# Performer layer: the half squares of the queries issued in two parts, the first ahead of the last query projection, the second behind the first tile's features

## What is computed

```python
def softmax_kernel(x, proj, is_query):
    norm = x.shape[-1] ** (-0.25)
    ratio = proj.shape[0] ** (-0.5)
    xp = jnp.einsum('bhnd,md->bhnm', x * norm, proj)
    diag = jnp.sum(jnp.square(x), axis=-1, keepdims=True) * 0.5 * (norm * norm)
    if is_query:
        stab = jnp.max(xp, axis=-1, keepdims=True)
    else:
        stab = jnp.max(xp, axis=(-1, -2), keepdims=True)
    return ratio * (jnp.exp(xp - diag - stab) + EPS_K)
...
qp = softmax_kernel(q, proj, is_query=True)
kp = softmax_kernel(k, proj, is_query=False)
k_sum = jnp.sum(kp, axis=2)
denom = jnp.einsum('bhnm,bhm->bhn', qp, k_sum)
ctx = jnp.einsum('bhnm,bhnd->bhmd', kp, v)
out = jnp.einsum('bhnm,bhmd->bhnd', qp, ctx) / denom[..., None]
```

## Time and profile before

| what | value |
|---|---|
| median of 3 runs | 2508.66 us |
| lowest and highest run | 2501.77 and 2509.47 us |
| the profiled execution's own time | 2511.11 us |
| its span | 2509.4 us |
| PE busy | 2360.6 us, 94% of the span |
| DVE, ACT, POOL busy | 1791.1, 1291.6, 701.0 us (71, 51, 28%) |
| mean granted clock of PE over the span | 0.97 of full speed |

### The profile page before, as it was taken

The page is one execution under the profiler, slowest core; times in us unless marked ns, Lnnn a source line. Parts: engine busy times, 40 slices in busy tenths (PEclk is TensorE's granted clock), DMA queues, the critical chain, the costliest instruction groups (busy, mean ns, idle before and its releaser), DMA issues.

```text
span 2509.4 us, 43786 instructions
## 1 busy us (share of the span) xinstructions
PE 2360.6 (94%) x16024; PEld 2182.2 (87%) x16024; DVE 1791.1 (71%) x3323; ACT 1291.6 (51%) x2027; POOL 701.0 (28%) x468
## 2 busy tenths in 40 slices
PE   7999995899999969999999999998999999999999
PEld 6888885899999968988988988987988998899998
DVE  5776775899999866565575574665788787877774
ACT  4445443344444325464464554564666665655554
POOL 1111111444454423023123122122344442321110
PEclk9999997999999989999999999996999999999999
DMA  5000000000000000000000000002000010000001
GB/s 182 0 0 0 0 0 20 1 0 0 0 0 0 1 17 1 13 8 13 13 4 17 13 4 17 8 13 81 26 18 22 20 50 28 1 26 26 25 25 34
DMA packets 43259, 45.69 MB, mean 18 GB/s; under 512 B 3120, under 2 KB 41904, under 8 KB 43184
## 3 DMA queue, kind: packets, MB, share of 16 engines
q1 hardware_dynamic: 43184, 44.69, 5.5%
HBM read 27.90 MB, written 16.78 MB: 18 GB/s over the span
## 4 chain that ended last, share of the span: by engine, by line
PE 51%; DVE 5%; issue 3%; ACT 2%; POOL 1%; DVEq 0%; ACTq 0%; POOLq 0%
PE m_ps_z L1859 12%; PE p_ps_a L1641 4%; PE p_ps_feat L279 4%; PE p_ps_a L1698 4%; PE p_ps_feat L281 3%; PE p_ps_feat L280 3%; PE m_ps_wide L279 3%; PE m_ps_wide L281 3%; PE m_ps_wide L280 3%; PE p_ps_a L1579 2%; PE p_ps_turn L1685 2%; PE m_ps_wide L1837 1%; PE m_ps_wide L1838 1%; PE m_ps_n L1820 1%; PE p_ps_b L279 1%
## 5 line engine op out<-in xcount | busy, mean ns | idle before, releaser
L1951 DVE TENSOR_TENSOR m_a_lo<-m_a,m_a_hi 128x512 fp32r<-128x512 f32 x256 | 201.2, 803 | 144.0 <-ACT m_a_hi L1911 140.1
L1859 PE MATMUL m_ps_z<-m_w_hi,m_a_hi 128*128 128x256 f32 x1024 | 290.7, 284 | 1.5 <-DVE m_a_lo L1951 0.9
L1859 PE MATMUL m_ps_z<-m_w_hi,m_a_lo 128*128 128x256 f32 x1024 | 288.0, 281 | 0.0
L1859 PEld LDWEIGHTS m_ps_z<-m_w_hi,m_a_hi 128*128 128x128 f32 x1024 | 192.3, 188 | 13.5 <-DVE d_w_lo L2468 1.9
L1859 PEld LDWEIGHTS m_ps_z<-m_w_hi,m_a_lo 128*128 128x128 f32 x1024 | 192.7, 188 | 0.0
L1907 ACT ACTIVATE m_a<-m_ps_wide,d_b,d_w_gain 128x512 f32<-128x512 f32 x128 | 99.8, 780 | 135.8 <-PE m_ps_wide L281 131.7
L1324 POOL TENSOR_TENSOR p_kf<-p_kf,p_k_shift 128x1024 f32<-128x1024 f32 x64 | 119.4, 1903 | 155.5 <-DVE p_k_shift L1459 155.5
L1859 PE MATMUL m_ps_z<-d_w_lo,m_a_hi 128*128 128x256 f32 x512 | 144.7, 283 | 0.0
L1859 PE MATMUL m_ps_z<-m_w_lo,m_a_hi 128*128 128x256 f32 x512 | 143.6, 280 | 0.0
L1641 PE MATMUL p_ps_a<-p_ctx_pair,p_kf 128*128 128x34 f32 x1024 | 128.4, 283 | 0.0
L1641 PEld LDWEIGHTS p_ps_a<-p_ctx_pair,p_kf 128*128 128x128 f32 x1024 | 127.7, 203 | 0.4
(11 more groups left out here) (350 smaller groups left out, 8027.4 us busy)
## 6 DMA issues: line engine op xcount, KB each, us to landing
residual<-in_x SPq DMA_DIRECT2D x8, 1024.0 KB, 11.8
attn<-p_attn SPq DMA_DIRECT2D x32, 256.0 KB, 2.2
m_attn<-attn SPq DMA_DIRECT2D x16, 512.0 KB, 3.8
out<-residual SPq DMA_DIRECT2D x16, 512.0 KB, 2.9
raw_weights<-in_d_q SPq DMA_DIRECT2D x2, 1024.0 KB, 7.2
m_attn<-in_d_scale SPq DMA_DIRECT2D x3, 512.0 KB, 4.0
raw_weights<-in_m_w1T SPq DMA_DIRECT2D x1, 1024.0 KB, 5.0
raw_weights<-in_m_w2T SPq DMA_DIRECT2D x1, 1024.0 KB, 7.9
```

The costliest lines, as they stand in the source:

```text
L1859: mm = pe.matmul(z, a, w[:, f, :], start=(f == 0 and k == 0 and j % 2 == 0), stop=(f == FC - 1 and k == 2), skip_group_check=True)
L1951: dve.tensor_tensor(self.a2[1][:, f, :], self.a[f % RING][:, :], self.a2[0][:, f, :].bitcast(F32), ALU.subtract).then_inc(self.a_lo, 1)
```

## The change

In the tail of the Performer layer PE's program is reordered. The first half of the queries' half squares (rows of fills 0 and 1) is issued before the last query projection, the second half (fills 2 and 3) behind the features of tile 0. The wait for the keys' half squares to have been copied moves with the first half. Tile 0's features now wait for the low parts of fills 0 and 1 alone (`kq_lo` at b * 8 + 6) and tile 1's for all four, where both waited for all four. DVE's, ACT's, POOL's and SP's programs are the same.

```diff
@@ -1666,17 +1666,18 @@
                 project("q", 2)
                 pe.wait_ge(stab_ready, b + 1)
                 pe.matmul(ps_b[:, 0:HEADS], ones[:, :], stab_diag[:, :], start=True, stop=True).then_inc(stab_spread, 1)
+                pe.wait_ge(halfsq_copied, 2 * b + 1)
+                half_squares(b, ps_a, 1, 0)
                 project("q", 3)
-                pe.wait_ge(halfsq_copied, 2 * b + 1)
-                for half in range(2):
-                    half_squares(b, ps_a, 1, half)
                 for i in range(TB + 2):
                     if i < TB:
                         if i < 2:
-                            pe.wait_ge(kq_lo, b * 8 + 8)
+                            pe.wait_ge(kq_lo, b * 8 + 6 + 2 * i)
                         else:
                             pe.wait_ge(q_shifted, b * TB + i - 1)
                         features(i).then_inc(qf_done, 1)
+                    if i == 0:
+                        half_squares(b, ps_a, 1, 1)
                     if i >= 2:
                         pe.wait_ge(q_exp, b * TB + i - 1)
                         if i >= 3:
```

## The result

| | before | after |
|---|---|---|
| median of 12 runs | 2508.22 us | 2513.53 us |
| lowest and highest | 2501.77, 2509.99 | 2511.99, 2514.82 |
| profiled execution, its span | 2511.11, 2509.4 | 2513.51, 2511.8 |

The account below looks back on a forecast made before the run. PE, busy 94% of the span, was read as the bound, with tile 0's add held to POOL's boundaries; +1.86 + 1.86 - 1.87 - 0.53 = +1.3 us on 2508.66 gave 2510.0 us, "same"; range 2503 to 2517.

Parts of the forecast that it names:

- Nothing to take away on PE: PE through one tail: no wait there for the reorder to remove; same matmuls, same 6.5 us sum.
- PE waits 0.1 us: Tile 0's features just cover ACT's square of fill 3; if short, PE waits 0.1 us.
- DVE 0.33 us later: Tile 0's maximum on DVE starts at 1080.47 instead of 1080.14 us, held by the copy of both halves.
- First boundary missed, second reached: Tile 0's add ends at POOL subtraction boundaries (7.9, 9.8, 11.6 us after `k_shift`); ready at 8.00, it ends at 9.8.
- The rival in which the second is missed: Low-clock tails: tile 0's add goes to the third boundary, +1.86 us each; 2517.4 with four, 2521.2 with six; chance 0.12.
- that in which the first is caught: Tile 0's add starts at or before 7.87 us: 2495.1 in all eight tails, 2502.6 in four; chance 0.07.
- Clock: PE's clock behind the half squares falls less often than in six of eight tails; bounds none and six, four taken.
- new idle time: Rival: PE waits for tile 0's subtraction, clock falls, 0.53 us per batch, 2512.1; chance 0.2 together with no boundary matters.
- The sum: All eight tails at the second boundary against the profiled execution: +1.86 + 1.86 - 1.87 - 0.53 = +1.3 us.
- the median: Last step: profiled execution 2.45 us above the median of three runs, so median put at 2508.66 + 1.3 = 2510.0 us.
- such an execution: An execution like the profiled one before the change: 2511.11 + 1.3 = 2512.4 us forecast.

Follow-up runs that it names:

- the pair of doses: Three PSUM copies delaying DVE, added to the kernel with first half squares behind projection 3: 2515.24 to 2513.16 us (half squares in SBUF), 2493.65 to 2502.50 (in PSUM).

## Why the prediction was right, and where it was off

*Nothing to take away on PE.* Right: no wait went, one of 0.13 us came, as the "PE waits 0.1 us" had it.

*DVE 0.33 us later.* Right in sign and cause (the copy in one piece behind both halves; shown by the run with the copy in two), short in size: 8.21 against 7.67 in b = 1 is 0.54. The wait of 0.13 is a part of it, and from the copy's start to the maximum's it is 0.42 us, not 0.29 + 0.04.

*First boundary missed, second reached.* Right in all eight tails; with the low clock the add was ready at 9.54, where 9.59 was forecast. That agreement is luck: 9.59 was for a clock that falls behind all the half squares, and the 9.54 came of one that fell during projection 3. The rival in which the second is missed did not come about, nor that in which the first is caught: the order with the first half squares behind projection 3, ready at 7.98, shows how near that was. The mechanism, that the add is held by POOL and the hold is all of a step, is shown by the runs with one SBUF input and by the pair of doses.

*Clock.* A fall early in the tail came in two tails, not the four that I took, within the bounds of none and six, and behind the first half squares, not behind the second; and the "new idle time" rival was real as well: in b = 0, 3 and 6 the clock fell as PE waited for tile 0's subtraction, which cost 0.3 us in each distance (96.9 against 96.6 for b = 0 and 3, 96.2 against 95.9 for b = 6), where I had 0.53.

*The sum.* +1.3 us between profiled executions; measured 2513.51 - 2511.11 = +2.4. The first mark came 0.4 us earlier. From the first mark to the last it is 0.3 us less (676.79 to 676.51), where 1.86 - 1.87 - 0.53 = -0.5 was forecast. Two things are missing in that sum: the 0.3 us of b = 0 and 3, and b = 6, which I had as unchanged. It had the same extra 0.53 before as b = 2 (96.48 against 95.95, its distance at the second boundary with the clock high), and half of it went. From the last mark on it is 3.1 us more (2509.4 - 1653.89 = 855.5 against 2511.8 - 1653.22 = 858.6), where the last tail's boundary gave +1.86. The other 1.2 come later: DVE's instructions are 1.85 us later against the last mark up to 40 us behind it, 2.7 from 53 us on and 3.1 from 100 us on. In both kernels the clock falls at about 45 us and is low for most of the time until some 95 us behind the mark, and after the change it falls about 3 us earlier. Granted clock (the third number from the end) from 44 to 47 us behind the last mark, before and after:

```profile
1697.89:1700.89 3.00, 2.44 (x22) 2.26 (x21) 3.00 (x2) 2.51 (x6) 1.98 (x1) 1.00 1.12 351
...
1697.22:1700.22 3.00, 2.98 (x17) 2.68 (x16) 1.82 (x4) 0.81 (x2) 1.59 (x1) 0.59 1.03 320
```

That the earlier fall makes the 1.2 us is likely, not shown. The forecast had no term behind the tails.

*The step that went wrong is the last: the median.* I took the profiled execution's 2.45 us above the median as an offset that both kernels share. It isn't one. Before, the boundary of a tail depended on whether and where PE's clock fell, and the runs lie between 2501.8 and 2510.0 us. After, every tail of the profiled execution is at the second boundary, high clock or low, and all runs are at 2512 to 2515. The mean granted clock of the unprofiled runs bears this out in part. Of the 48 executions of before that were measured beside the experiments, the 15 below 2504 us had 0.972 to 0.974 and the 14 above 2508 us 0.969 to 0.972. The 12 after had 0.972 to 0.975, as the shortest of before, and took 2512 to 2515 us all the same. At which boundary the tails of those runs ended was not seen. For "such an execution" I had 2512.4, against 2513.51 measured. Carried over, the offset made 2510.0, so +1.3 us, where the medians moved by +5.3. A change that puts every tail at one boundary has to be compared with the whole spread of the runs before. With 0.27% it is "same" by a hair, and the interval lies on both sides of 0.3%.

## What to carry to other kernels

When a tiny instruction has a duration that varies tenfold in a trace, look at its end against the other engines' instruction edges before you cost a delay: if it is quantised, small delays are free up to an edge and cost a whole step beyond it, and the total time proves little about which part of an edit did it. Moving work out from between a producer and a consumer helps only if nothing behind both (here one copy of both halves) still ties them. And cost a change against the spread of the runs before, not against one profiled execution.

## What the runs showed of the hardware

A DVE add of 128x16 with both inputs in SBUF took 0.17 us alone and up to 1.92 us while POOL ran a 128x1024 subtraction in SBUF; with one input in PSUM it took 0.17 us throughout. I had expected that. Not expected was that plain SBUF-to-SBUF copies of 128x128 are held as well (5.37 us for three, against 0.94 us for three out of PSUM under the same POOL work). The Trainium skill (SBUF — State Buffer, section "Who interferes with whom") has both: copies can take the shared ports, and the later one is blocked in full. The 5.37 us agree. POOL's eight subtractions took 14.93 and 14.94 us in the two kernels, so the adds held nothing up on its side.

PE's granted clock fell from its upper to its lower level (2.4 to 1.2 GHz, shown as 1.00 and 0.50) in or behind 3.5 us of 16-column matmuls in six of eight tails before, although PE was busy throughout. It fell in none of 48 behind 1.7 us of them between 512-column matmuls, and in 19 of 40 (two of eight in the change) where those 1.7 us stood directly behind a small matmul and an idle time of 0.28 us. That is what stood ahead of the falls in these traces, not a rule for when it falls. Both levels were seen within one kernel at the same place of the program, so the place alone doesn't decide it.
